# An adaLN block and a rotation on one core: scores in padded 32-row groups, and a setup in another order

## What is computed

```python
ada = silu(c) @ W_ada + b_ada                    # six rows of 144 for each sequence
h = layernorm(x) * (1 + scale_msa) + shift_msa
qkv = (h @ W_qkv + b_qkv).reshape(b, l, 3, 16, 9)   # 16 heads of 9 channels
scores = einsum('blhd,bmhd->bhlm', q * 9**-0.5, k)
o = einsum('bhlm,bmhd->blhd', softmax(scores), v)
x = x + gate_msa * (o @ W_proj + b_proj)
x = x + gate_mlp * (gelu(h2 @ W_fc1 + b_fc1) @ W_fc2 + b_fc2)   # h2: second modulated norm
U, _ = qr(P)                                     # 144 x 64
v = silu(cond) @ W.T + b                         # 2016 entries for each sequence
A = skew(v)                                      # 64 x 64, v above the diagonal, -v below
R = expm(A)
x = x + einsum('btd,nd->btn', (x @ U) @ R - x @ U, U)
```

## Time and profile before

| | us |
|---|---|
| three runs | 362.82, 363.0, 363.6 (median 363.0) |
| the profiled execution, its own time | 363.15 |
| its span, first to last instruction | 361.4 |
| TensorE busy / weight loads busy | 318.2 (88%) / 245.4 (68%) |
| VectorE busy | 256.6 (71%) |
| ScalarE busy | 187.2 (52%) |
| GpSimd busy | 146.2 (40%) |
| mean granted TensorE clock | 0.948 of full |

### The profile page before, as it was taken

How to read it: one execution, slowest core, us unless ns; L and a number is a source line. 1 busy time by engine, 2 the same in 40 slices (tenths; PEclk the granted TensorE clock), 3 DMA queues, 4 the chain that set the end, 5 groups by cost and what they waited for, 6 DMA issues and landing times.

```text
span 361.4 us, 10608 instructions
## 1 busy us (share of the span) xinstructions
PE 318.2 (88%) x3935; PEld 245.4 (68%) x3935; DVE 256.6 (71%) x1063; ACT 187.2 (52%) x403; POOL 146.2 (40%) x421
## 2 busy tenths in 40 slices
PE   0598989889989899999999999999987957999995
PEld 0472668567877788787778777777776643467784
DVE  7381036688899989887786878988988576664243
ACT  1222464347766557567685676776762233623221
POOL 3512124235355454553543535545543508720000
PEclk9998765769999999999999999999999899999999
DMA  8817000000000000000000000000000000000013
GB/s 198 233 19 261 4 1 2 3 1 2 2 3 2 2 5 3 2 2 3 2 3 2 5 2 2 0 5 0 2 3 3 2 3 0 2 0 2 0 34 100
DMA packets 8765, 8.28 MB, mean 23 GB/s; under 512 B 1042, under 2 KB 8312, under 8 KB 8586
## 3 DMA queue, kind: packets, MB, share of 16 engines
q1 hardware_dynamic: 8006, 6.78, 6.5%
q10 hardware_dynamic: 708, 0.83, 0.8%
HBM read 6.40 MB, written 1.20 MB: 21 GB/s over the span
## 4 chain that ended last, share of the span: by engine, by line
PE 61%; DVE 18%; ACT 8%; issue 5%; POOL 4%; DMA 2%; ACTq 1%; DVEq 0%; POOLq 0%
PE bank L1255 5%; PE bank L1492 5%; PE bank L1284 4%; PE bank L1476 3%; PE bank L1318 3%; PE bank L1171 3%; PE bank L1273 3%; PE bank L1308 3%; PE bank L1300 3%; PE bank L1244 3%; PE bank L1245 2%; PE bank L1179 2%; PE bank L1274 2%; ACT KT L626 2%; PE bank L1263 2%
## 5 line engine op out<-in xcount | busy, mean ns | idle before, releaser
L440 POOL TENSOR_TENSOR root<-rec,mhalf 128x1 f32<-128x1 f32 x64 | 34.6, 540 | 107.5 <-DVE Z L922 107.5
L984 DVE TENSOR_REDUCE nmax<-bank 128x4 f32<-128x512 f32 x64 | 43.0, 672 | 34.5 <-PE bank L1263 34.2
L616 ACT ACTIVATE E<-bank 128x512 f32<-128x512 f32 x64 | 38.0, 594 | 40.6 <-PE bank L1274 40.2
L626 ACT ACTIVATE KT<-bank 64x512 bf16<-64x512 bf16 x64 | 37.5, 587 | 0.8
L1273 PE MATMUL bank<-QT,KT 128*128 128x128 bf16 x256 | 36.7, 224 | 0.0
L1274 PE MATMUL bank<-NMT,headsel 128*128 128x128 bf16 x256 | 36.3, 222 | 0.0
L1308 PE MATMUL bank<-Z,sel 128*128 128x128 f32 x128 | 29.5, 314 | 6.9 <-DVE Z L928 6.8
L1284 PE MATMUL bank<-E,V 128*32 128x128 f32 x512 | 27.9, 291 | 5.4 <-ACT E L616 5.4
L622 ACT ACTIVATE QT<-bank 128x512 bf16<-128x512 bf16 x32 | 19.0, 595 | 26.1 <-PE bank L1255 26.0
L1273 PEld LDWEIGHTS bank<-QT,KT 128*128 128x128 bf16 x256 | 24.3, 99 | 10.0 <-issue 10.0
L1308 PEld LDWEIGHTS bank<-Z,sel 128*128 128x128 f32 x128 | 20.9, 200 | 14.7 <-issue 13.6
(11 more groups left out here) (270 smaller groups left out, 827.5 us busy)
## 6 DMA issues: line engine op xcount, KB each, us to landing
gates<-gates_dram SPq DMA_DIRECT2D x1, 2304.0 KB, 8.4
x_all<-in_x_dram SPq DMA_DIRECT2D x4, 288.0 KB, 7.6
out_dram<-x_all SPq DMA_DIRECT2D x8, 144.0 KB, 2.0
wskew<-in_L_cond_W_dram SPq DMA_DIRECT2D x4, 283.5 KB
wada<-in_L_cond_W_ada_dram ACTq DMA_DIRECT2D x1, 432.0 KB
wfc1a<-in_L_cond_W_fc_dram SPq DMA_DIRECT2D x1, 288.0 KB
wfc2a<-in_L_cond_W_fc_dram SPq DMA_DIRECT2D x1, 288.0 KB
wproj<-in_L_cond_W_proj_dram SPq DMA_DIRECT2D x16, 5.1 KB
```

The costliest lines, as they stand in the source:

```text
L440: link(nc.gpsimd.tensor_tensor(root[:, at], rec[:, at], mhalf[:, 0:1], ALU.pow))
L616: nc.scalar.activation(E[:, q, :, :].rearrange("p i t -> p (i t)"), bank[4][:, :], ACT.Exp).then_inc(s_E, 1)
L626: nc.scalar.activation(KT[parity][n][own, p, :, :].rearrange("p g t -> p (g t)"), bank[2][own, 256:512].bitcast(BF16), ACT.Copy).then_inc( ...
L984: nc.vector.tensor_reduce(nmax[:, q % 2, 4 * (q // 2):4 * (q // 2) + 4], bank[3][:, :].rearrange("p (i m) -> p i m", i=4), AX.X, ALU.max, ...
```

## The change

**Scores.** q and k are stacked in f32, each head in 32 slots: nine channels, one slot for the negated maximum, zeros (`qstk`, `kstk`; three ACT copies straight out of PSUM, `stacked`). TensorE transposes four heads at once (`stack_T`: four transposes for the keys, four for the queries, and after the maxima the four query stacks once more with the maxima in slot 9, where the keys hold ones, `queries_again_T`). A head's scores are then one f32 product on 32 rows, and the four heads of a group stand on four row groups and write to four banks. Row maxima and exponentials are taken of 128 x 1024 in one operation, two of each an iteration in the place of four of 128 x 512. Both directions of the scores share the first 256 columns of banks 0 to 3.

**Values and division.** `V` carries a column of ones, so the sums come with the values; the result is copied, transposed back by two transposes (`heads_back`), and divided on DVE by a 128 x 16 reciprocal and one 128 x 144 product (`divided`); two transposes and two ACT copies (`oT1`, `oT2`) make the operand of a two-matmul projection.

```diff
-            def scores_T(q, b, parity):
-                wait(pe, s_NMT, b + 1)
-                wait(pe, s_E, 4 * b + q)
-                for i in range(4):
-                    dst = bank[4][:, 128 * i:128 * i + 128]
-                    mm(dst, KT[parity][q // 2][:, q % 2, i, :], QT[parity][q // 2][:, i, :], start=True, stop=False)
-                    ins = mm(dst, headsel[:, q % 2, 4 * (q // 2) + i, :], NMT[:, :], start=False, stop=True)
+            def scores_T(b, g):
+                pe.wait_ge(s_QM, b + 1)
+                pe.wait_ge(s_max, min(2 * b + 3 + g, 2 * B))
+                wait(pe, s_E, 2 * b + g)
+                for j in range(2):
+                    for r in range(4):
+                        rows = slice(32 * r, 32 * r + 32)
+                        ins = mm(bank[r][:, 128 * j:128 * j + 128], KT[b % 3][rows, 2 * g + j, :], QM[rows, 2 * g + j, :],
+                                 start=True, stop=True)
                 ins.then_inc(s_ST, 1)
```

```diff
-                dve.wait_ge(s_O, b + 1)
-                dve.wait_ge(s_div, b + 1)
-                TT(ON[:, :, :].rearrange("p q t -> p (q t)"), Osb[:, :], bank[6][:, :], ALU.mult).then_inc(s_on, 1)
+                dve.wait_ge(s_Ot, b + 1)
+                wait(dve, s_OnT, b)
+                slots = bank[6][:, 256:512].rearrange("p (h s) -> p h s", h=H)
+                link(nc.vector.reciprocal(rsum[:, :].rearrange("p (h a) -> p h a", a=1), slots[:, :, D:D + 1]))
+                TT(ON[:, :].rearrange("p (h d) -> p h d", h=H), slots[:, :, 0:D],
+                   rsum[:, :].rearrange("p (h a) -> p h a", a=1).to_broadcast([128, H, D]), ALU.mult).then_inc(s_on, 1)
```

```diff
+        FIRST = 5
+        STEPS = {}
+        for b in range(0, B + 1):
+            for q in range(4):
+                if FIRST + len(STEPS) <= RD and (q < 3 or b % 4 < 3):
+                    STEPS[b, q] = FIRST + len(STEPS)
```

```diff
+            sp.wait_ge(k_fill, 8)
+            for i in range(RD - 1):
+                at = (RD - 1) * i - i * (i - 1) // 2 - i
+                sp.wait_ge(s_v, min(4, (at + RD - 2) // 504 + 1))
+                for p in range(2):
+                    sp.dma_start(A0[64 * p + i:64 * p + i + 1, :, :], v[p:B:2, at:at + RD]).then_inc(s_win, 16)
...
-            def windows(first, last):
-
-                for i in range(first, last):
-                    at = (RD - 1) * i - i * (i - 1) // 2 - i
-                    for p in range(2):
-                        ins = mm(bank[4][64 * p:64 * p + RD, NC * i:NC * i + NC], v[:, at:at + RD],
-                                 ident[0:B, p:B:2], start=True, stop=True)
...
+            modulations(bank[6], (0, 1))
+            pe.wait_ge(s_Z, 4)
+            step_rows(0)
+            inputs_T(0)
+            modulations(bank[3], (3, 4))
+            pe.wait_ge(s_ldq, 48)
+            qkv(0)
+            step_rows(1)
+            gate_rows()
+            keys_T(0)
+            queries_T(0)
+            generator_weights(0)
+            wait(pe, s_QT, 1)
+            inputs_T(1)
+            step_rows(2)
+            generator_weights(1)
+            step_rows(3)
+            generator_weights(2)
+            step_rows(4)
+            generator_weights(3)
+            for b in range(0, B + 2):
+                attention(b)
```

More of the change, by code:

```diff
@@ L1053, in products_evacuated @@
+            generator_weights(2)
+            eliminations(3)
+            generator_weights(3)
+            eliminations(4)
+            for b in range(0, B + 2):
+                attention(b)
             def products_evacuated():
@@ new lines, in attention @@
+            def attention(b):
+                if scoring(b):
+                    scores(b, 0)
+                step(b, 0)
+                if closing(b):
+                    values(b - 2, 1)
+                if b == B + 1:
+                    transposed_again(0)
+                if prepares(b):
+                    qkv(b + 1)
+                if weighing(b):
+                    scores_T(b - 1, 0)
+                step(b, 1, heads_back if closing(b) else None)
+                if b == B + 1:
+                    transposed_again(1)
+                if prepares(b):
+                    keys_T(b + 1)
+                    queries_T(b + 1)
+                if b == B:
+                    U_parts(b, 0)
+                if scoring(b):
+                    scores(b, 1)
+                if weighing(b):
+                    values(b - 1, 0)
+                generator_stage(b)
+                if b == B:
+                    U_parts(b, 1)
+                step(b, 2)
+                if closing(b):
+                    bank5_read(b)
+                    normalized_T(b - 2)
+                if b == B + 1:
+                    more_squarings()
+                    transposed_again(2)
+                if weighing(b):
+                    scores_T(b - 1, 1)
+                step(b, 3, projection if closing(b) else None)
+                if b == B + 1:
+                    transposed_again(3)
+                if scoring(b):
+                    if closing(b):
+                        pe.wait_ge(s_oT, 2 * b - 2)
+                    else:
+                        bank5_read(b)
+                    queries_again_T(b)
+                if normalizing(b):
+                    bank4_read(b)
+                    inputs_T(b + 2)
+                if b == B:
+                    U_parts(b, 2)
+                if b == 1:
+                    pe.wait_ge(s_ldp, 16 * 3)
@@ L1448, in products @@
+            step_rows(4)
+            generator_weights(3)
+            for b in range(0, B + 2):
+                attention(b)
             def products():
                 pe.wait_ge(s_R, 1)
-                pe.wait_ge(s_pr, B + 1)
+                pe.wait_ge(s_pr, B)
                 pe.wait_ge(m_hT, 4)
```

1121 lines of the change are left out of this document (548 added, 573 removed).

## The result

The changed kernel takes 395.8 us (median of four runs, 394.03 to 400.4) against 363.3 for the kernel before in the same series. The ratio is 1.088 with a 95% interval of 1.083 to 1.092: it is slower by 9%, where 322 us and "faster" were forecast. The profiled execution is the longest of the four, 400.4 us with a span of 398.6; the other three are at 394.0 to 396.4, with 395.2 in their middle, and what an experiment on this kernel gains is counted from 395.2.

What follows compares the result with a forecast made beforehand. TensorE and VectorE, both nearly full and chained, bound the kernel. Setup 37.2, iterations 205.1 (matrix work included), window wait 1.3, end 14.5 and MLP and rotation 62.4 give 320.5 us of span; with 1.75 outside, 322, range 308 to 344.

Steps and rivals of the forecast that it cites:

- the clock rival: Attention: TensorE's clock falls, a third of the time at the low level, 19 us more, 341 us; chance 0.22.
- the walk through the order: Four-step iteration followed on VectorE in written order, with waits of 0.9 and 0.5 us for TensorE: 11.9 us.
- The window transfers: Ahead of `triangles` in iteration 3: 126 transfers at 0.3 us each on SP's queue, a wait of 1.3 us.
- The rival: Window transfers over 0.75 us each: iteration 3 waits over 40 us, the gain is gone; chance of over 335: 0.04.
- Matrix work: Iterations 0 to 14: matrix operations first fill VectorE's waits, the rest lengthens iterations by 21.5 us in all.
- "wrong" signs: TensorE records twice as long in the attention, tens of us of wait before `triangles`, or calls of 1 us and more.
- A four-step iteration with squaring: Iterations 12 to 14: 11.9 us for the four-step chain plus 1.0 us of squaring, 12.9 us each.
- The call of row groups: Scores on TensorE: eight f32 products in two rounds of 0.3 us, 0.6 a call, bounds 0.5 and 0.8.
- The maxima: VectorE in an iteration: two maxima of 1024 columns at 1.15 us each, in place of four of 0.54.
- The setup: Before the attention: TensorE starts at 7.0 us, first scores at 37.2 instead of 46.8; bounds 33 and 41.
- The last iterations: Last three iterations: 24.7 us instead of 33.3, one of 10.2 with scores and 14.5 for the others.
- MLP and rotation: The stage after the attention: stays at 62.4 us.

Runs made afterwards that it cites:

- e3_both_halves: The kernel after with 63 window transfers of 16 rows, each filling both halves, in place of 126 of eight: 357.1 us, 0.978 of before.
- e5: e3_both_halves with 8, 6, 8 and 8 identity products ahead of the bank 5 waits in iterations 4, 5, 9 and 10: 348.5 us, 0.959 of before.
- e7_order: e3_both_halves with scores_T ahead of the wait for bank 5 and the division ahead of the statistics: 350.7 us, 0.964 of before.
- e11: e7_order with 6, 4, 6 and 6 identity products ahead of scores_T in iterations 4, 5, 9 and 10: 342.7 us, 0.944 of before.
- e6_fill_all: e5 with identity products also in the setup and the last iterations: 345.5 us, 0.953 of before.

## Why the iterations are longer: waits for a bank, then half the clock

In iteration 5 of the kernel after, TensorE forms the rows of its third step (L1414, L1417) and then waits for bank 5, in which `norms` (L1229) lies. VectorE reads it with `fro` only behind the step and the normalisation. TensorE's timeline, then VectorE's:

```profile
161.16 0.39 PE L1229 MATMUL banks<-rowsq,halves 128*128 128x8 f32 x2
161.41 0.47 PE L1414 MATMUL banks<-Z,ident 128*128 128x128 f32 x2
161.71 0.33 PE L1417 MATMUL banks<-Z,ident 128*128 128x64 f32 x2
164.14 0.45 PE L1394 MATMUL banks<-ident,ON 128*128 128x128 f32 x1 [2.10 <-issue]
```

```profile
162.08 0.17 DVE L886 RECIPROCAL rec<-banks 128x1 f32<-128x1 f32 x1 [0.61 <-PE banks L1417]
...
163.62 0.35 DVE L856 TENSOR_SCALAR xn<-x_all,mv,rstd 128x144 f32<-128x144 f32 x1
163.88 0.16 DVE L735 COPY fro<-banks 128x8 f32<-128x8 f32 x1
```

TensorE stands 2.1 us. After it the same records are longer (0.45 us for one transpose that takes 0.30 at 285.55). The same wait comes in iterations 4, 9 and 10, with 2.62, 2.62 and 2.64 us in the kernel with half the transfers. A part of what iteration 6 is too long is the same wait for bank 4, without a fall of the clock, which is 1.00 in the whole of it. TensorE waits there until VectorE has read that bank and made `flag`:

```profile
184.45 0.30 PE L1299 MATMUL banks<-ident,xn 128*128 128x128 f32 x1 [1.39 <-DVE flag L826]
```

These are the stretches of 2 us about the wait of iteration 4 in the kernel with half the transfers:

```profile
100.00:102.00 2.00, 0.85 (x14) 0.64 (x9) 1.08 (x8) 0.00 (x0) 0.06 (x1) 1.00 0.00 0
102.00:104.00 2.00, 0.53 (x2) 0.19 (x2) 1.33 (x4) 0.00 (x0) 0.88 (x3) 0.81 0.00 0
104.00:106.00 2.00, 2.00 (x21) 1.72 (x20) 0.00 (x0) 1.06 (x3) 0.00 (x0) 0.50 0.00 0
106.00:108.00 2.00, 2.00 (x11) 1.99 (x10) 1.55 (x10) 0.39 (x1) 0.55 (x1) 0.50 0.00 0
108.00:110.00 2.00, 2.00 (x21) 1.35 (x20) 0.84 (x4) 1.27 (x3) 1.24 (x3) 0.50 0.00 0
```

Some 2.6 us of idle time are followed by 7 us at 1.2 GHz (clock 0.50), in which TensorE is busy without a pause and VectorE isn't.

**Products that compute nothing.** If the idle time lowers the clock, work that nobody needs must make the kernel faster.

```
+                if b in (4, 5, 9, 10):
+                    pe.wait_ge(s_max, 2 * b + 2)
+                    pe.wait_ge(s_E, 2 * b - 1)
+                    filled(0, 6 if b == 5 else 8)      # mm(bank[0][:, 0:128], ident, ident)
                 if closing(b):
                     bank5_read(b)
```

> e3_both_halves with 8, 6, 8 and 8 products of the identity with itself (0.29 us each, 1.7 to 2.3 us together) into bank 0 ahead of the four waits of iterations 4, 5, 9 and 10 (2.6, 2.1, 2.6 and 2.65 us idle before bank 5 is free again in e3_both_halves). They add work and take nothing away. Theory (the idle time brings the low level, and the low level is what makes these iterations long): the stretches at 1.2 GHz behind those waits (about 7, 3, 12 and 4 us in e3_both_halves) go, half of 26 us is gained, 357 falls to 344 to 347. Rival (the level has another reason, or the stretches at 1.2 GHz only fill time that VectorE sets): 356 to 359.

> e5 with such products also in the setup (seven into bank 6 ahead of each of two waits of 2.4 us, after which e3_both_halves shows 1.2 GHz from 28 to 42 us) and in the last iterations (five into bank 4 or 5 ahead of the values of iterations 15 and 16, 3, 5 and 5 into bank 0 in the last one; 1.2 GHz there from 266 to 274 and 277 to 297 us). Theory of the clock: of these 42 us a third to a half is gained, 330 to 338. Rival: like e5 or, as the added products stand on the path, up to 3 us longer.

Measured: 348.5 us (0.959 of before, 0.953 to 0.965) and 345.5 us (0.953, 0.948 to 0.958), from 357.1. Thirty products more and 8.6 us less: with the idle time filled, the granted clock is 1.00 in the whole of iterations 4, 5, 9 and 10, where it was 0.81, 0.89, 0.75 and 0.81. The idle time lowers the clock, and the low clock is on the path. The same stretches with the products:

```profile
100.00:102.00 2.00, 2.00 (x27) 1.93 (x24) 1.05 (x7) 0.00 (x0) 0.00 (x0) 1.00 0.00 0
102.00:104.00 2.00, 1.22 (x13) 0.84 (x15) 1.37 (x4) 0.01 (x1) 0.94 (x3) 1.00 0.00 0
104.00:106.00 2.00, 2.00 (x28) 1.88 (x29) 0.77 (x6) 1.43 (x3) 0.00 (x0) 1.00 0.00 0
```

Iterations 4, 5, 9 and 10 take 15.1, 13.9, 17.9 and 15.2 us for 18.1, 15.3, 20.7 and 18.4. Iteration 6, without such products, takes 16.9 for 15.5 and has 3 us at the low level instead: the clock fell there, around its wait of 1.48 us for bank 4. The first was expected at 344 to 347 and is little above it; the second was expected at 330 to 338 and isn't there: with the products in the setup and in the last iterations only 3 more us are gained. The mean clock rises from 0.941 to 0.975, which is an estimated 24 us less at the low level (twice the missing share of the clock, times the span: 41 against 17 us). So this low clock was worth an eighth of its time, where the four waits gave back over a quarter (0.899 to 0.941, an estimated 31 us, for 8.6). That the waits there remain whatever the clock is would explain it, but no run shows it.

**The order.** `scores_T` ahead of the wait, and the division ahead of the statistics.

```
+                if weighing(b):
+                    scores_T(b - 1, 1)
                 if closing(b):
                     bank5_read(b)
                     normalized_T(b - 2)
-                if weighing(b):
-                    scores_T(b - 1, 1)
...
-                    if q == 1 and within(b, 3, B + 1):
-                        statistics(b - 3)
                     if q == 1 and closing(b):
                         divided(b - 2)
+                    if q == 1 and within(b, 3, B + 1):
+                        statistics(b - 3)
```

> e3_both_halves with two changes of order: TensorE forms scores_T (0.67 us) ahead of the wait for bank 5 instead of behind it, and VectorE does the division of an iteration ahead of its statistics (0.22 us), since TensorE waits 0.88 us in every iteration for ON. Theory (these waits stand on the path): 14 x 0.2 + 4 x 0.67 = 5.5 us less, 351 to 352. Rival (VectorE's own line sets the iteration): 356 to 358.

Measured: 350.7 us, 0.964 of before (0.957 to 0.971), from 357.1: 6.4 us for 5.5 expected. The waits are on the path. But the sum behind the 5.5 doesn't hold term by term: 14 times 0.2 us were to come from the division, but iterations 12 and 13 are 0.2 us shorter, 2 is unchanged, and 3, 7 and 11 are 0.2 to 0.3 us longer. The gain lies in iterations 4, 5, 9 and 10, which lose 7.9 us together in the trace. The four waits fall to 1.96, 1.44, 1.96 and 1.98 us. The low stretch behind the one of iteration 4 shrinks from three slices of 2 us to one, so a part of this gain is the clock's again.

**Both.**

> e7_order with 6, 4, 6 and 6 products ahead of scores_T in iterations 4, 5, 9 and 10. If the two gains add (6.4 and 8.5 of 357.1): 342. If they are the same gain, since both fill the same wait: 348 to 350.

> e11 with the products of e6_fill_all in the setup and the last iterations as well. If these add as they did (3.0 us): 339. If the order leaves nothing for them: as e11.

Measured: 342.7 us (0.944, 0.938 to 0.951) and 338.1 us (0.933, 0.928 to 0.939, six runs). The gains add, 357.1 - 6.4 - 8.6 = 342.1, where one and the same gain would have left 348 to 350. The first of these kernels also tells the order from the clock: against the four fills alone, iterations 4, 5, 9 and 10 are 0.7 to 1.1 us shorter each, 3.4 together, with a clock of 1.00 in both. That is the order's own part there; the rest of the 7.9 is then the clock's. The second is the fastest kernel of the study, 7% under the kernel before. Its stretches, from setup to MLP:

```profile
0.00:39.00 39.00, 27.91 (x162) 21.33 (x162) 17.00 (x110) 7.30 (x15) 13.48 (x41) 1.00 0.61 166
39.00:266.00 227.00, 197.34 (x2725) 147.41 (x2725) 168.08 (x733) 99.60 (x213) 74.70 (x226) 0.99 0.01 3
266.00:275.00 9.00, 6.68 (x37) 6.00 (x38) 4.34 (x16) 1.80 (x5) 1.12 (x3) 0.62 0.01 2
275.00:337.80 62.80, 57.42 (x416) 38.96 (x414) 31.98 (x100) 20.28 (x41) 16.73 (x33) 1.00 0.07 20
```

The clock is 0.99 in the attention with all transposes and all products on 32 rows in place. So it is not these that lower it. The Trainium skill's sentence on transposes (TensorE: Matmul & The Clock Gate, PE-mode transpose) gave the clock rival a part of its chance; here 18 transposes an iteration, among other products, leave the clock at 1.00 where no long wait stands beside them.

## What is left: more work of TensorE, and waits

At full clock and without the window wait, 338 us are still 16 over the forecast. TensorE's timeline of iteration 13 in the kernel after, at clock 1.00, shows it (start, duration with the pipeline's depth, line, records):

```profile
278.21 0.73 PE L1361 MATMUL banks<-QM,KT 32*128 32x128 f32 x16
278.87 0.49 PE L1414 MATMUL banks<-Z,ident 128*128 128x128 f32 x2
...
280.55 0.73 PE L1349 MATMUL banks<-KT,QT 32*128 32x128 f32 x16
282.15 0.65 PE L1378 MATMUL banks<-E,V 128*32 128x128 f32 x16 [0.88 <-DVE ON L925]
282.73 1.15 PE L1181 MATMUL banks<-Xm,Ym 64*64 64x64 f32 x32
...
284.74 0.49 PE L1414 MATMUL banks<-Z,ident 128*128 128x128 f32 x2
```

A call of scores takes 0.66 us to the next operation (278.21 to 278.87), or 0.73 to its own end where TensorE has to wait behind it; four are 2.8 where 2.4 was taken. The rows of the four steps take 0.49, 0.66, 0.47 and 0.58 us to the next operation, 2.2 for 1.8. `qkv` takes 1.65 for 1.52. Without the 2.0 us of squaring the iteration has 10.6 us of TensorE work, not 9.4. And it has a wait of 0.88 us ahead of the values, which the walk through the order didn't have: the values go to one half of bank 6, and the program lets them wait for `ON`, which VectorE reads from its other half behind the step.

Iteration 2 has four steps and no product for the matrices, and its row shows what this work does by itself:

```profile
72.01:84.90 12.89, 10.52 (x142) 7.83 (x138) 11.26 (x59) 6.00 (x13) 5.04 (x16) 1.00 0.02 4
```

TensorE is busy for 10.5 us here too, and still the iteration takes 12.9 us, 1.4 less than forecast. So the larger work alone doesn't make an iteration too long. In iteration 13 the squaring stands between the second maximum and the third step, and VectorE waits 2.40 us for that step's rows (at 285.44 us), where the forecast had no wait and charged 1.0 us for the squaring. In the fastest kernel 8.7 of the 11.6 us that iterations 0 to 13 are over the forecast lie in iterations 4, 6, 9 and 10, and 3.7 in 11 to 13; 2, 3, 7 and 8 are 2.0 us below it together. Waits for a bank of 1.39 us (iteration 6) and 1.26 us (iteration 9) still stand there at a clock of 1.00.

## Where the prediction was right and where it failed

- **The window transfers: the step that failed.** The price of 0.3 us came from a one-row load of a bias and from W_proj; it measured 0.70 from start to start. Both rows are transfers of other shape, and none of before moves eight pieces of one partition each into a single partition. The rival stated the mechanism and nearly its threshold (over 0.75 us each, a wait of over 40 us); the wait was 43.3, at 0.70. But its chance of 0.04 rested on "The rows say half of that at most". This was no bound, since the rows were of another shape, and it wasn't what the queue said either: the load of `bfc`, in the same timeline, holds it for 0.59 us, and the four of `x_all` for 1.5 each. With 126 equal operations on one queue each 0.1 us of price is 12.6 us of time, so the range had to carry a factor of two here. From 1.3 to 43.3 us this term is 42 of the 73 us that were missed; taking the transfers away gave 38.1.
- **Matrix work: mis-sized.** It was forecast to stretch 4, 5, 6, 9 and 10 by 0.5 to 2.0 us each over an iteration without it. They are 3 to 5 us longer than forecast. The sum took the lengths of operations and where they fill VectorE's idle time, but not the other side: the program doesn't let TensorE write bank 5 again (in iteration 6, bank 4) before VectorE's operation has read it, and this operation stands behind a step in VectorE's order. It is the question "who waits for that", which was asked of SyncE's queue and not of the bank.
- **The clock rival: right in its mechanism.** Its "wrong" signs, records of longer duration in the attention, are there. Forecast was the low level for a third of the time and 19 us; after the window wait is taken away, the clock is 0.90 in the mean, which is an estimated fifth of the time at the low level, and the added products gain 8.6 and 3.0 us. What lowers the clock in the pipeline are above all four waits of 2.1 to 2.7 us and the loose last iterations, not the 1.6 us of idle time that iterations 11 to 13 have at most, in pieces of up to 0.9, which leave it at 1.00.
- **A four-step iteration with squaring: mis-sized.** 11.9 was forecast without matrix work, 12.9 with squaring; it is 14.2, with 1.2 us more TensorE work, the wait of 0.88 and 2.0 us of squaring where 1.0 was charged. The 11.9 itself was never measured, since every iteration carries something beside it; iteration 2, at 12.9 for 14.3, speaks for it. VectorE was to be the fuller engine. In iteration 13 it is busy for 9.6 us, near the 9.8 forecast, and TensorE for 12.6.
- **The call of row groups: right, at 0.66** between the bounds of 0.5 and 0.8. A drain that would lift a call to the upper bound isn't seen: two rounds of 0.29 are 0.58 by the estimate from the earlier trace rows, so about 0.1 us a call is left for both changes of mode.
- **The maxima: right.** 1.14 us from start to start for 1.15 forecast (1.22 with the pipeline's depth).
- **The setup: right in sum.** TensorE starts at 6.2 us (7.0 forecast), the first scores come at 38.4 (37.2 forecast, 36 to 38 as the sign of being right; 37.4 in the kernel without transfers).
- **The last iterations: mis-sized.** From the `qkv` at 290.78 to the end of the attention it takes 45.2 us; 35 were forecast. With the clock kept up and the order changed it is 41.6 (233.4 to 275.0).
- **MLP and rotation: right**, 62.6 for 62.4.
- **Sums that don't come out as written.** The bounds of 0.5 and 0.8 us a call are 0.4 less and 0.8 more an iteration than 2.4, not 1.6 and 0.4; TensorE's terms add up to about 9.6 us, not 9.4, and VectorE's to 9.6, not 9.8. None of this is near the size of the miss.

Added up for the kernel without the transfers, against 319.2 us of span without the window term: setup +0.2, iterations 0 to 13 +27.1 (209.1 for 182.0), the rest of the attention +9.8, MLP +0.2. That is 37.3, and its span of 356.6 is 37.4 above. (An iteration is counted from its `qkv`, 2.3 us behind its first scores.) In the fastest kernel the iterations 0 to 13 take 193.6: the clock and the part of the waits that was removed were 15.5 of the 27.1, and 11.6 are left for TensorE's work and the waits that stand there still. How they share it stays open, since no run changes the work alone.

## To carry to other kernels

A price for an operation that is repeated a hundred times on one queue must come from a row of its own shape: number of pieces, contiguous or not, one partition or many. Without such a row, let the dear rows of the queue set the range and not the cheap ones (0.59 us stood beside 0.28 and 0.36 here), and divide the time until the result is asked for by the number of repetitions (45 us here, for 126: 0.36 us each). When work is placed beside a tuned chain, follow the memory it borrows until it is given back: the reader's place in its engine's order decides how long the writer stands idle, and an idle time of 2.1 to 2.64 us was followed here by 3 to 12 us at half the clock.

## What had not been expected of the hardware

- A transfer of 2 KB to one partition holds the queue for 0.25 us when its source is one contiguous piece (2 packets), and 0.62 to 0.64 us when it is eight (16 packets); one row of 256 or 512 bytes out of `v` is cut into 32 packets and costs 0.59. Yet a load of sixteen rows to sixteen partitions holds it for 0.31 only.
- Thirty products added to TensorE in four waits of 2.10 to 2.64 us made the kernel 8.6 us faster.
- Eight products on four row groups between operations of other shape cost 0.66 us, hardly more than two undisturbed rounds (an estimated 0.58, twice a quarter of the 1.14 us in the earlier trace rows).
